# Softmax maxima that reach q's rows through DRAM instead of through a transpose on PE

## What is computed

```
q = apply_rope(x @ Wq.T + bq);  k = apply_rope(x @ Wk.T + bk);  v = x @ Wv.T + bv
scores = softmax(q @ k.T / sqrt(256), axis=-1)      # 16 heads, 4096 x 4096 each
out = scores @ v
x = layernorm(x + out @ Wo.T)
x = layernorm(x + ffn(x))
```

## Time and profile before

| what | us |
|---|---|
| median of 3 runs | 3414.24 (3413.72 to 3414.84) |
| the profiled execution, its own time | 3415.28 |
| its span, first to last instruction | 3413.7 |
| granted TensorE clock, mean of the span | 0.983 of full speed |
| attention: first group of maxima to last exponentials | 119 to 2732 |
| one unit in the middle | 79.07 |

### The profile page before, as it was taken

One profiled execution on the slowest core, in us unless ns is written; L12 is line 12 of the kernel. 1 busy time (PEld: TensorE's weight loads), 2 busy tenths in 40 slices (PEclk: granted clock), 3 DMA queues, 4 the chain that ended last, 5 costly groups with the idle time before them and its releaser, 6 DMA issues.

```text
span 3413.7 us, 66851 instructions
## 1 busy us (share of the span) xinstructions
PE 3345.3 (98%) x28054; PEld 1528.5 (45%) x28054; DVE 2985.4 (87%) x3116; ACT 2490.2 (73%) x4521; POOL 128.0 (4%) x288
## 2 busy tenths in 40 slices
PE   9689999999999999999999999999999999999998
PEld 5333333333333333333333333333333288888887
DVE  8999999999999999999999999999999145555554
ACT  5248888888888888888888888888888922222222
POOL 0000000000000000000000000000000000000000
PEclk9679999999999999999999999999999999999999
DMA  4200000000000010001001000000002020000000
GB/s 157 76 4 12 13 12 13 25 15 17 25 12 14 11 62 12 13 13 62 13 11 31 14 12 12 14 13 12 13 8 95 9 96 26 26 26 26 26 13 13
DMA packets 47618, 92.04 MB, mean 27 GB/s; under 512 B 9922, under 2 KB 21828, under 8 KB 47140
## 3 DMA queue, kind: packets, MB, share of 16 engines
q1 hardware_dynamic: 40628, 72.07, 6.6%
q0 software_dynamic: 6688, 15.68, 1.6%
HBM read 69.62 MB, written 28.84 MB: 29 GB/s over the span
## 4 chain that ended last, share of the span: by engine, by line
PE 91%; DVE 5%; ACT 2%; issue 1%; DMA 0%; SPq 0%; DVEq 0%; ACTq 0%
PE sums L680 32%; PE scores L782 25%; PE acc L1121 17%; PE wide L658 13%; DVE group_max L895 2%; PE tok L1168 2%; ACT probs L866 1%; PE tok L1094 1%; DVE pair L305 1%; ACT mixed L846 1%; DVE item L316 1%; DVE pair L313 1%; DVE item L312 1%; PE scores L748 0%; DVE k_all L330 0%
## 5 line engine op out<-in xcount | busy, mean ns | idle before, releaser
L895 DVE TENSOR_REDUCE group_max<-wide 128x2 f32<-128x1024 f32 x2048 | 2473.3, 1223 | 18.2 <-PE wide L658 11.6
L866 ACT ACTIVATE probs<-scores 128x512 f32<-128x512 f32 x4046 | 2199.8, 597 | 294.5 <-PE scores L782 43.6
L680 PE MATMUL sums<-probs,v_all 128*17 128x256 f32 (+1 forms) x16120 | 1279.3, 389 | 7.2 <-ACT mixed L846 6.3
L782 PE MATMUL scores<-q_sb,k_all 51*128 51x512 f32 x3968 | 988.7, 495 | 6.7 <-ACT probs L866 5.7
L658 PE MATMUL wide<-k_all,q_sb 48*128 48x512 f32 x4096 | 851.2, 412 | 30.1 <-DVE group_max L895 25.5
L782 PEld LDWEIGHTS scores<-q_sb,k_all 51*128 51x128 f32 x3968 | 370.7, 183 | 843.2 <-ACT probs L866 829.9
L680 PEld LDWEIGHTS sums<-probs,v_all 128*17 128x17 f32 x16120 | 267.3, 95 | 748.0 <-issue 368.3
L658 PEld LDWEIGHTS wide<-k_all,q_sb 48*128 48x128 f32 x4096 | 397.6, 190 | 68.9 <-DVE group_max L895 62.8
L1234 ACT ACTIVATE whole_hid<-acc,scale 128x512 f32<-128x512 f32 x128 | 84.6, 688 | 286.3 <-PE acc L1121 286.1
L1121 PE MATMUL acc<-hid_b,h2T 128*128 128x512 f32 x1024 | 234.9, 390 | 0.0
L1121 PE MATMUL acc<-hid_a,first_h1T 128*128 128x512 f32 x1024 | 233.4, 389 | 0.0
(11 more groups left out here) (121 smaller groups left out, 1075.1 us busy)
## 6 DMA issues: line engine op xcount, KB each, us to landing
q_sb<-q_parts SPq DMA_DIRECT2D x192, 64.0 KB, 2.5
heads<-mixed SPq DMA_DIRECT2D x128, 34.0 KB
xt<-in_xT SPq DMA_DIRECT2D x8, 512.0 KB, 4.4
q_parts<-k_all SPq DMA_DIRECT2D x8, 512.0 KB, 3.3
q_parts<-parts SPq DMA_DIRECT2D x8, 512.0 KB, 3.3
w_words<-in_h1T POOLq DMA_DIRECT2D x32, 128.0 KB, 2.3
w_words<-in_h2T POOLq DMA_DIRECT2D x32, 128.0 KB, 2.3
heads_sb<-heads SPq DMA_DIRECT2D x16, 256.0 KB
```

Of the source, the lines that this page charges most:

```text
L680: last = pe.matmul(sums[32 * j:32 * j + HD + 1, cols], v_all[:, kt, g, j], probs[(kt * HG + j) % RING][:, cols], start=(kt == 0 and cols.s ...
L782: pe.matmul(scores[(s + e) % BANKS][:], k_all[rows, g * GP + j, n // HG * P:(n // HG + 1) * P], q_sb[g][rows, j], start=True, stop=True).t ...
L866: act.activation(probs[n % RING][:], bank, ACT.Exp, scale=INV_SCALE)\
L895: dve.reduce_max(group_max[:, n], wide[n % 2][:], AX_X).then_inc(wide_free, 1)
```

## The change

`top` is no longer transposed by PE. Pool splits it as it lies, 128 x 16, and negates the parts; SP stores them to a DRAM tensor `turn` (128 x 48 floats), waits for that, and issues six DMAs that read one 4-byte element after another (stride 192 bytes) and write them into the rows of q. PE's transpose, ACT's copy and the extra place in the rotation of the banks are gone. `LEAD` is 8.

```diff
-        LEAD = 6
-        TURN_AT = TILES - (LEAD - 1) * HG + 2
-        SLOTS = TILES + 1
+        LEAD = 8
...
-        shift = sb("shift", [QT, P])
-        shift_rest = sb("shift_rest", [QT, P])
-        shift_parts = sb("shift_parts", [QT, 3, P], BF16)
-        shift_rows = sb("shift_rows", [QT, 3, P], F32R)
+        top_rest = sb("top_rest", [P, QT])
+        top_parts = sb("top_parts", [P, 3, QT], BF16)
+        shift_parts = sb("shift_parts", [P, 3, QT], F32R)
...
+        turn_dram = nc.dram_tensor("turn", [2, P, 3 * QT], F32, kind="Internal").ap()
...
                 sp.wait_ge(part_step, (u + 2) * ROUNDS)
+                sp.dma_start(turn_dram[u % 2], shift_parts[:].rearrange("s a r -> s (a r)").bitcast(F32)).then_inc(turned, 16)
+                sp.wait_ge(turned, 16 * (u + 1))
                 for e in range(PAIR):
                     for a in range(3):
                         at = e * HALF + SHIFT_ROW + a
+                        src = turn_dram[u % 2, :, a * QT + e * GP * TT:a * QT + (e + 1) * GP * TT].rearrange("s r -> r s")
                         row = q_sb[g][at:at + 1].rearrange("o j (t s) -> o (j t) s", t=TT)
-                        sp.dma_start(row.bitcast(F32), shift_rows[e * GP * TT:(e + 1) * GP * TT, a].bitcast(F32)).then_inc(shift_in, 16)
+                        sp.dma_start(row.bitcast(F32), src, allow_slow_non_contiguous=True).then_inc(shift_in, 16)
...
-            def split_shift(u):
+            def split_top(u):
...
-                pool.wait_ge(shift_in, u * 96 + 96)
+                pool.wait_ge(top_ready, u + 1)
...
-                pool.tensor_copy(shift_parts[:, 0], shift[:]).then_inc(part_step, 1)
+                pool.tensor_copy(top_parts[:, 0], top[:]).then_inc(part_step, 1)
...
+                pool.wait_ge(shift_in, u * 96 + 96)
                 pool.wait_ge(part_step, base + 4)
                 pool.sem_inc(waited, 1)
-                pool.tensor_copy(shift_rows[:], shift_parts[:]).then_inc(part_step, 1)
+                pool.tensor_scalar(shift_parts[:], top_parts[:], -1.0, None, ALU.mult).then_inc(part_step, 1)
...
-            def max_turn(u, bank, done):
-
-
-                pe.wait_ge(top_ready, u + 1)
-                pe.transpose(scores[bank][0:QT, 0:P], top[:], ident[:]).then_inc(done, 1)
...
-                    turn_at(n + PAIR)
...
-                    if n == TURN_AT and not last:
-                        act.wait_ge(scored, u * SLOTS + n + 1)
-
-                        act.wait_ge(part_step, (u + 2) * ROUNDS)
-                        act.activation(shift[:], scores[n % BANKS][0:QT, 0:P], ACT.Copy, scale=-1.0)\
-                            .then_inc(exps_done, 1)
...
-                if u == 1:
-                    dve.wait_ge(first_turn, 1)
-                elif u > 1:
-                    dve.wait_ge(scored, (u - 2) * SLOTS + TURN_AT + 1)
+                if u > 0:
+                    dve.wait_ge(part_step, (u + 1) * ROUNDS)
```

More of the change, by code:

```diff
@@ L479, in attend @@
         top_ready = sem("top_ready")
-        first_turn = sem("first_turn")
+        turned = sem("turned")
         part_step = sem("part_step")
@@ L515, in attend @@
         flip = [wide[1][:, f] for f in range(FT)]
-        last_banks = [scores[b][:] for b in range(BANKS)] + [wide[0][:, e] for e in range(PAIR)]
+        turn_dram = nc.dram_tensor("turn", [2, P, 3 * QT], F32, kind="Internal").ap()
+        last_banks = [scores[((UNITS - 1) * TILES + b) % BANKS][:] for b in range(BANKS)] + [wide[0][:, e] for e in range(PAIR)]
         def pieces_beside(u):
             return range(len(PIECES) * u // UNITS, len(PIECES) * (u + 1) // UNITS)
-        def slot(n, turn=True):
-            return n + 1 if turn and n >= TURN_AT else n
         @block.sync
@@ L611, in load_words @@
                     pool.dma_start(w_words[i % WORDS][:], words).then_inc(words_in[i % WORDS], 16)
[L613 removed]
+            def split_top(u):
                 base = (u + 1) * ROUNDS
[L617 removed]
+                pool.wait_ge(top_ready, u + 1)
                 pool.wait_ge(part_step, base)
                 pool.sem_inc(waited, 1)
[L620 removed]
+                pool.tensor_copy(top_parts[:, 0], top[:]).then_inc(part_step, 1)
                 pool.wait_ge(part_step, base + 1)
[L622 removed]
+                pool.tensor_tensor(top_rest[:], top[:], top_parts[:, 0], ALU.subtract).then_inc(part_step, 1)
                 pool.wait_ge(part_step, base + 2)
                 pool.sem_inc(waited, 1)
[L625 removed]
+                pool.tensor_copy(top_parts[:, 1], top_rest[:]).then_inc(part_step, 1)
                 pool.wait_ge(part_step, base + 3)
[L627 removed]
+                pool.tensor_tensor(top_parts[:, 2], top_rest[:], top_parts[:, 1], ALU.subtract)\
                     .then_inc(part_step, 1)
+                pool.wait_ge(shift_in, u * 96 + 96)
                 pool.wait_ge(part_step, base + 4)
                 pool.sem_inc(waited, 1)
[L631 removed]
+                pool.tensor_scalar(shift_parts[:], top_parts[:], -1.0, None, ALU.mult).then_inc(part_step, 1)
             load_words(0)
             load_words(1)
[L636 to L637 removed]
+            split_top(0)
             load_words(2)
             for u in range(1, UNITS):
[L641 to L642 removed]
+                split_top(u)
                 if u + 2 < UNITS:
@@ L660, in max_group, with sum_over @@
                 last.then_inc(wide_ready, 1)
-            def max_turn(u, bank, done):
-                pe.wait_ge(top_ready, u + 1)
-                pe.transpose(scores[bank][0:QT, 0:P], top[:], ident[:]).then_inc(done, 1)
             def max_start(c, g):
                 pe.wait_ge(q_in[g], c * (16 * PLACES) + 16 * PLACES)
-            def sum_over(u, g, kt, turn=True, cols=slice(0, CH)):
+            def sum_over(u, g, kt, cols=slice(0, CH)):
                 if kt == 0 and cols.start == 0:
@@ L676, in sum_over @@
                 if cols.start == 0:
-                    pe.wait_ge(exps_done, u * SLOTS + slot(kt * HG + HG - 1, turn) + 1 + BANKS)
+                    pe.wait_ge(exps_done, u * TILES + kt * HG + HG + BANKS)
                 for j in range(HG):
@@ L752, in last_unit @@
                     if kt > 0:
-                        sum_over(u, g, kt - 1, False)
+                        sum_over(u, g, kt - 1)
                     else:
@@ L775, in score_pair @@
                 def score_pair(n):
-                    s = slot(n, left > 0)
-                    pe.wait_ge(exps_done, u * SLOTS + s + PAIR)
+                    s = u * TILES + n
+                    pe.wait_ge(exps_done, s + PAIR)
                     j = n % HG // PAIR
@@ L783, in score_pair @@
                                   q_sb[g][rows, j], start=True, stop=True).then_inc(scored, 1)
-                def turn_at(n):
-                    if n == TURN_AT and left > 0:
-                        pe.wait_ge(exps_done, u * SLOTS + n + 1)
-                        max_turn(u + 1, n % BANKS, scored)
                 def sums_of_previous(kt, cols=slice(0, CH)):
                     if kt > 0:
-                        sum_over(u, g, kt - 1, left > 0, cols)
+                        sum_over(u, g, kt - 1, cols)
                     elif not first:
-                        sum_over(u - 1, (g - 1) % NG, KT - 1, True, cols)
+                        sum_over(u - 1, (g - 1) % NG, KT - 1, cols)
                 pe.wait_ge(shift_in, u * 96 + 192)
@@ L831, in _ @@
             last_unit(NG - 1)
-            sum_over(UNITS - 1, NG - 1, KT - 1, False)
+            sum_over(UNITS - 1, NG - 1, KT - 1)
         @block.scalar
@@ L836, in _ @@
             act.sem_inc(probs_free, RING // HG)
-            act.wait_ge(first_turn, 1)
-            act.activation(shift[:], scores[0][0:QT, 0:P], ACT.Copy, scale=-1.0).then_inc(exps_done, BANKS)
+            act.sem_inc(exps_done, BANKS)
             def take_sums(c, g):
@@ L859, in unit @@
                         act.activation(fc.root[:], fc.spread[:], ACT.Sqrt).then_inc(root0_done, 1)
-                    s = slot(n, not last)
-                    act.wait_ge(scored, u * SLOTS + s + 1)
+                    s = u * TILES + n
+                    act.wait_ge(scored, s + 1)
                     if n % HG == 0:
```

6 lines of the change are left out of this document (2 added, 4 removed).

## The result

| what | before | with the change |
|---|---|---|
| median, us | 3414.54 (4 runs, 3413.72 to 3414.93) | 4054.3 (4 runs, 4041.45 to 4078.27) |
| ratio | 1 | 1.1878, 95% interval 1.1853 to 1.1902 |
| profiled execution, us | 3415.28 | 4059.92 |
| its span, us | 3413.7 | 4058.4 |
| granted clock, mean | 0.983 | 0.895 |

The kernel became 640 us slower. The forecast was 3405.0, in a range of 3400 to 3600.

A forecast was written before the change was run, and what follows sets the result against it. PE, busy 98% of the span, was taken as the bound. Turns removed (-13.6 us), a longer opening (+4.5) and cheaper pairs in unit 30 (-0.1) gave -9.2 us: 3405.0 us against 3414.24, range 3400 to 3600.

The forecast's parts named there:

- The packets: Six loads from `turn`: 768 packets on each of 8 engines at 12 ns, 9.2 us; 15.9 ns the point of decision.
- hidden: Likeliest case: the new path ends before PE's scores need it, 3.0 us to spare; 3405.0 us, chance 0.50.
- What is removed: On PE: 31 turns of 0.44 us, transpose plus wait for a bank, go; -13.6 us.
- The opening: Before unit 0's scores: 16 groups of unit 1 instead of 12, at DVE's pace of 1.133 us; +4.5 us.
- The sum if hidden: Whole kernel, new path hidden: -13.6 + 4.5 - 0.1 = -9.2 us, so 3405.0 against 3414.24.
- The time there is: From the end of `top` to the first scores that need it: 18.5 us.
- Store and wait: SP's store to `turn` and the wait for it: 3.2 us, from the store of inverse sums.
- The start: Opening: unit 0's first scores near 210.4, leaving 17.0 us for a chain of 15.5.
- SP, Pool and DVE: Other work on these engines: the new waits and the stores and loads queued behind cost nothing.
- The clock after a wait: PE after idling before a unit: 6.9 us at 1.2 GHz, 2.9 us lost.
- Far too late: Loads from `turn`: 38.6 ns a packet, 17.4 us late each unit, then a lower clock; 4034 us, chance 0.23.
- A little late: Loads from `turn`: 16 to 20 ns a packet; at 19.3, PE waits 2.6 us a unit, 3575 us; chance 0.20.

The follow-up runs named there:

- e6_two_hops: Changed kernel, but three loads bring the 4-byte pieces into 16 SBUF partitions, then six whole-row loads fill q; 3405.92 us, in eleven later runs 3408.26.
- e7_turn_in_store: Changed kernel, but the store to DRAM does the transposition in 6144 pieces, and six loads read 4096 bytes in one piece; 3709.19 us.
- e1_lead8_only: The kernel before with only LEAD changed, from 6 to 8; 3420.18 us, ratio 1.0018.
- e2_whole_rows: Changed kernel, but each of the six loads reads 4096 bytes in one stretch, leaving out the transposition; 3407.52 us, ratio 0.9978.
- e9_eight_rows: As `e6_two_hops`, but the first hop is six loads of 1024 pieces, each into 8 partitions; 3555.82 us.

## Why the prediction was wrong

**The step that failed is "The packets".** It took a price for each packet and divided the pieces by the engines: 768 x 12 ns = 9.2 us, with ends at 7 and 19.3 ns. The loads took 31.2 us from issue to scores, 40 ns for each of 768. The fault is the form of the term, more than its price: where nothing held the packets up, in the first microsecond, they took 9.0 ns each, less than the 12. What the sum had at nothing is the pace of the place that is written. With 4, 8 and 16 engines the time differs by 13% at most; what counts is 6144 pieces x about 5 ns into one partition at a time. All the rows behind the price had data in pieces of 256 bytes or more, and none had many pieces for one partition. The prediction wrote that "none of them is 4 bytes from scattered places", and in pricing the packets looked at where pieces are read from; the reads were cheap (`e6_two_hops`) and the writes dear. Its far rival did name the small writes into one partition's row, beside the scattered reads, but gave them no price of their own.

The price itself wasn't bad for what it measured: spread over 16 partitions a packet took 10.5 ns, where 12 was taken. Two of the rows behind it were read too simply. The 109 packets of the earlier trace rows are 94 pieces of 256 bytes and 15 semaphore writes, the 88 of the earlier trace rows are 80 pieces of 256 bytes, 3 of 2048 and 5 semaphore writes. In both the pieces of 256 bytes took 17.5 or 17.6 ns and the semaphore writes, which have 4 bytes, 9.0. So "nothing shows a packet below 16" was not so, and a better price lay in the trace; it would have made "hidden" look safer still.

The Trainium skill gives about 10.5 ns a packet (DMA: Bandwidth & Descriptors, Bandwidth, Measured). Read as a time for each engine, the two-hop run gives the same figure; read for all engines together, as the prediction weighed it, it would have given an estimated 64.5 us, and the change took 31.2. Its advice to rearrange an elementwise DMA away (the same page, Rules for kernel authors) held for the change and for `e7_turn_in_store`, but `e6_two_hops` makes as many pieces and hides them.

**What stood, step by step:**

- *What is removed.* 31 turns, -13.6 us; from `e1_lead8_only` to `e2_whole_rows` -12.7.
- *The opening.* +4.5 us; `e1_lead8_only` measured +5.7, with an interval of 2.7 to 9.6.
- *The sum if hidden.* 3405.0 us; `e2_whole_rows` took 3407.52 and the two-hop kernel 3408.26.
- *The time there is.* 18.5 us; 18.4 measured.
- *Pool.* 0.2 + 1.7 us; from the end of `top` at 296.09 to the end of its last operation at 297.96 it was 1.9.
- *Store and wait.* 3.2 us; 297.98 to 299.49 is 1.5. The relative in the earlier trace rows was too slow.
- *Engines.* 8 a load; right.
- *The start.* First scores of unit 0 were forecast near 210.4; in `e2_whole_rows` they came at 212.00. In the change they came later, at 232.74, after a wait of 20.50 us: the opening had no more room than any unit.
- *SP, Pool and DVE.* Nothing, which held, though SP was held 21.3 us in issuing; nobody waited for it.
- *The clock after a wait.* 2.9 us; 3.7 a unit. The row behind it had 6.9 us at the lower clock after a wait of 2.38 us; in unit 1 of the change, after 16.21 us, it lasted over 7 us.

**The rivals.** "Far too late" came true, with 0.23: 4034 forecast, 4054 measured. Its 38.6 ns came from doubling the largest row, so its size was luck, but its mechanism (a wait of 17.4 us a unit, then the clock) is what the waits show: 16.9 a unit. It counted 31 waits and left out the one in the opening, of 20.50 us, which is about what the forecast lacks. "A little late" had the point right from which it decides; `e9_eight_rows`, with 1.9 us of waiting, ended at 3556, near that rival's 3575, though this was reached by another kernel. The range stopped at 3600 because the far rival was put at what may be left out. With no row of the kind at hand, 0.5 for "hidden" was too much: the margin of 3.0 us rested on one guessed price times 768.

## What to carry to other kernels

Before work is moved from the bound engine into element-wise DMAs, count the pieces and look at the partition in which they land: a row of one partition filled piece by piece took 5 to 6 ns a piece here with 4, 8 and 16 engines, the same pieces over 16 partitions 1.2, and a second hop with whole rows cost less than it saved. Let such a path have some microseconds to spare: most waits of PE over 1 us were followed by slow matmuls here, and these cost more than the waits. Don't read a DMA engine's busy share as work done, nor a mean packet time as a price. And where the nearest rows differ from the new transfer in the thing that may decide, the range has to hold the far case too.

## What the runs showed of the hardware that was not expected

- 4-byte pieces into one partition: 31.8 us (4 engines), 31.2 (8), 35.2 (16) for 6144, from DRAM; 35.0 from SBUF. Into 8 partitions 11.7 us, into 16 partitions 7.1. Whether the partition itself is the limit, or engines that write side by side in the same stretch of it, wasn't told apart; four engines did no worse than sixteen, and one alone was not run.
- In the change the first thousand pieces went at 9.0 ns a packet, and the last 5.5 us of the wait have no packet on record.
- 6144 pieces written to scattered places in DRAM: 20.5 us.
- Such loads slow others: 128 KB of words landed after 11.5 us instead of 2.3.
- With `LEAD` 16, PE stopped up to 3.44 us without a releaser while they ran. Fetches of 16 KB of instructions took 6.3, 5.7 and 4.2 us before the three stops; that they are the cause isn't proven.
- 1.53 us of waiting was followed by matmuls at the lower clock; with `LEAD` 7 the waits for loads, 14.9 us in all, went with 21.9 us more of PE's busy time. A wait of 1.42 us was followed by the full clock.
